# One product per pair of heads and one sum per sequence on VectorE, in a cross-attention kernel

## The reference, cut to what matters

```python
xn = (input - mu) * rsqrt(var + EPS) * gamma + beta        # per sequence
q, kv = Wq @ xn + bq, Wkv @ context + bkv                  # 8 heads
att = softmax(q^T k * c ** -0.5)                           # 256 x 256 per head
y = att @ v
out = input + Wo @ y + bo
```

## Time and profile before

| What | us |
|---|---|
| Three runs: lowest, median, highest | 228.17, 229.04, 229.39 |
| Profiled execution, first to last instruction (span) | 228.2 |
| TensorE busy, in the profiled execution | 208.6 |
| VectorE busy | 199.3 |
| ScalarE busy | 181.1 |
| GpSimd busy | 160.3 |

### The profile page before, as it was taken

How to read it: one execution, slowest core, us unless ns; L and a number is a source line. 1 busy time by engine, 2 the same in 40 slices (tenths; PEclk the granted TensorE clock), 3 DMA queues, 4 the chain that set the end, 5 groups by cost and what they waited for, 6 DMA issues and landing times.

```text
span 228.2 us, 7194 instructions
## 1 busy us (share of the span) xinstructions
PE 208.6 (91%) x2511; PEld 179.9 (79%) x2511; DVE 199.3 (87%) x589; ACT 181.1 (79%) x371; POOL 160.3 (70%) x157
## 2 busy tenths in 40 slices
PE   6968878799999999999999998999999999999872
PEld 6857757588888798889888887888888888887761
DVE  3589987879898999899999999999999998989765
ACT  2374586787889988898889888989897979888880
POOL 5135185777987877789788887789686869776460
PEclk9975897999999999999999999999999999999998
DMA  5964137480767566566665665656657656442000
GB/s 134 261 272 93 27 82 174 107 184 14 164 141 160 131 153 142 132 141 151 140 153 122 160 151 121 151 127 154 142 127 166 149 133 143 93 94 62 13 3 23
DMA packets 31090, 29.04 MB, mean 127 GB/s; under 512 B 4240, under 2 KB 29840, under 8 KB 31056
## 3 DMA queue, kind: packets, MB, share of 16 engines
q1 hardware_dynamic: 30224, 28.07, 52.4%
q10 hardware_dynamic: 832, 0.53, 1.0%
HBM read 3.80 MB, written 1.05 MB: 21 GB/s over the span
## 4 chain that ended last, share of the span: by engine, by line
PE 41%; POOL 20%; issue 13%; ACT 11%; DVE 11%; ACTq 2%; POOLq 0%; DVEq 0%
POOL p_lo L773 19%; PE ps_sc L522 6%; PE ps_max L546 6%; PE ps_sc L523 5%; PE ps_z L479 4%; ACT p_full L678 4%; DVE neg_max L894 4%; ACT p_hi L675 3%; PE ps_z L481 3%; PE ps_z L480 3%; PE ps_z L414 3%; PE ps_m L589 2%; PE ps_t L497 2%; PE ps_m L590 2%; DVE z_sum L910 2%
## 5 line engine op out<-in xcount | busy, mean ns | idle before, releaser
L773 POOL TENSOR_TENSOR p_lo<-p_full,p_hi 128x512 f16<-128x512 f32 x122 | 139.9, 1163 | 42.3 <-ACT p_full L678 41.2
L675 ACT ACTIVATE p_hi<-ps_sc 128x512 f16<-128x512 f32 x128 | 77.9, 608 | 18.3 <-PE ps_sc L523 15.9
L894 DVE TENSOR_REDUCE neg_max<-ps_max 128x2 f32<-128x512 f32 x128 | 85.9, 677 | 6.9 <-PE ps_max L546 6.8
L678 ACT ACTIVATE p_full<-ps_sc 128x512 f32<-128x512 f32 x128 | 78.7, 615 | 0.0
L522 PE MATMUL ps_sc<-t_a,c_seq 128*128 128x256 f32 x256 | 71.2, 300 | 3.5 <-issue 2.6
L523 PE MATMUL ps_sc<-t_b,c_seq 65*128 65x256 f32 x256 | 67.3, 284 | 0.0
L479 PEld LDWEIGHTS ps_z<-u_hi,p_hi 128*128 128x128 f16 x512 | 46.4, 97 | 12.8 <-issue 8.2
L479 PE MATMUL ps_z<-u_hi,p_hi 128*128 128x65 f16 x512 | 53.0, 195 | 2.2 <-DVE p_lo L930 1.9
L522 PEld LDWEIGHTS ps_sc<-t_a,c_seq 128*128 128x128 f32 x256 | 49.2, 192 | 5.9 <-issue 4.6
L480 PE MATMUL ps_z<-u_lo,p_hi 128*128 128x64 f16 x512 | 52.8, 193 | 0.0
L481 PE MATMUL ps_z<-u_hi,p_lo 128*128 128x65 f16 x512 | 52.7, 194 | 0.0
(11 more groups left out here) (108 smaller groups left out, 233.9 us busy)
## 6 DMA issues: line engine op xcount, KB each, us to landing
t_a<-t_a SPq DMA_DIRECT2D x90, 128.0 KB, 2.4
t_b<-t_b SPq DMA_DIRECT2D x30, 128.0 KB, 2.5
x_seq<-x_hi SPq DMA_DIRECT2D x15, 128.0 KB, 2.4
c_pad<-c_hi SPq DMA_DIRECT2D x30, 64.0 KB, 2.1
c_seq<-c_hi SPq DMA_DIRECT2D x15, 128.0 KB, 2.4
x_res<-x_tiles SPq DMA_DIRECT2D x4, 256.0 KB, 6.7
out<-x_res SPq DMA_DIRECT2D x16, 64.0 KB, 2.0
x_seq<-x_lo SPq DMA_DIRECT2D x15, 64.0 KB, 2.1
```

What stands on the lines that cost most here:

```text
L675: nc.scalar.activation(p_hi[:, buf, :, :].rearrange("p t s -> p (t s)"), scores, ACT.Exp).then_inc(act_phi, 1)
L678: nc.scalar.activation(p_full[:, head % 2, :], scores, ACT.Exp).then_inc(act_p, 1)
L773: nc.gpsimd.tensor_tensor(p_lo[:, buf, :, :].rearrange("p t s -> p (t s)"), p_full[:, head % 2, :], p_hi[:, buf, :, :].rearrange("p t s -> ...
L894: nc.vector.tensor_reduce(to, ps_max[:, unit % 2, :].rearrange("p (t s) -> p t s", t=KT), X, ALU.max, negate=True).then_inc(dve_max, 1)
```

## The change

Per pair, VectorE multiplies all four blocks by their reciprocals in one instruction, with each reciprocal broadcast over 64 elements, and writes the results to a new tile `z_heads`, in which the eight heads of one output element lie side by side. Behind the last pair's product, one reduction over these eight gives `z_sum`. A new semaphore, `dve_zpart`, counts the products; `dve_zsum` now counts sequences. TensorE's value products wait for the product of the pair that had their bank, and no longer for its addition. The last pair's reduction waits for the four products and for the transpose of two sequences before.

```diff
+        z_heads = sb("z_heads", [P, 2, KT * C, H], fp32)
...
-                    need(pe, dve_zsum, (m * PAIRS + first // 2 - 1) * 2 * KT)
+                need(pe, dve_zpart, m * PAIRS + first // 2 - 1)
...
-                    for k in range(2):
-                        head = first + k
-                        for qt in range(KT):
-                            total, part, scale = z_sum[:, m % 2, qt, :], sums[:, qt, k, 0:C], inv_sum[:, pair % 2, qt * 2 + k:qt * 2 + k + 1]
-                            if head == 0:
-                                nc.vector.tensor_scalar(total, part, scale, 0.0, ALU.mult, ALU.add).then_inc(dve_zsum, 1)
-                            else:
-                                dve.wait_ge(dve_zsum, (m * H + head - 1) * KT + qt + 1)
-                                nc.vector.scalar_tensor_tensor(out=total, in0=part, scalar=scale, in1=total, op0=ALU.mult,
-                                                               op1=ALU.add).then_inc(dve_zsum, 1)
...
+            def add_values(m, first):
...
+                dve.wait_ge(dve_inv, m * PAIRS + pair + 1)
+                need(dve, dve_zsum, m - 1)
+                to = z_heads[:, m % 2, :, first:first + 2].rearrange("p (t c) k -> p t k c", t=KT)
+                nc.vector.tensor_tensor(to, sums[:, :, :, 0:C], inv.broadcast_to([P, KT, 2, C]), ALU.mult).then_inc(dve_zpart, 1)
+                if first == H - 2:
+                    need(dve, pe_y, m - 1)
+                    dve.wait_ge(dve_zpart, (m + 1) * PAIRS)
+                    nc.vector.tensor_reduce(z_sum[:, m % 2, :, :].rearrange("p t c -> p (t c)"), z_heads[:, m % 2, :, :], X,
+                                            ALU.add).then_inc(dve_zsum, 1)
```

```diff
+                reduce_max(n + 2, 2)
+                p_low(n, 7)
+                u_low(n + 1, 1)
```

More of the change, by code:

```diff
@@ L317, in run, with run_cycles, turn_of, fresh @@
                     step(n, h)
+        def run_cycles(step, cycle):
+            for n in range(-1, FIRST_CYCLE):
+                for h in range(H):
+                    step(n, h)
+            for n in range(FIRST_CYCLE - 1, N + 2):
+                cycle(n)
+        def turn_of(m, k):
+            return k if m == 0 else PAIRS + 2 * (m - 1) + k
+        def fresh(done, kind, index, within=True):
+            if not within or index < done.get(kind, 0) or kind == 't' and index >= PAIRS + 2 * (N - 1):
+                return False
+            done[kind] = index + 1
+            return True
         def chunk(c):
@@ L446, in transpose_max @@
             def transpose_max(m, part):
+                if not fresh(done, 'mt', m + 1 if m else part, m < N):
+                    return
                 rows = H * KT
@@ new lines, in values @@
+            def values(m, first):
+                if not fresh(done, 'values', m * PAIRS + first // 2, 0 <= m < N):
+                    return
+                bank = first // 2 % 2
+                if first == 0:
+                    pe.wait_ge(dve_ulo, 2 * (m + 1))
+                if m == 0 and first < 4:
+                    pe.wait_ge(dve_tlo, T_EARLY)
+                need(pe, dve_zpart, m * PAIRS + first // 2 - 1)
+                lo_done(pe, m, first)
+                lo_done(pe, m, first + 1)
+                for head in (first, first + 1):
+                    buf = head % P_BUFS
+                    for qt in range(KT):
+                        qs = slice(qt * P, (qt + 1) * P)
+                        z0 = (qt * 2 + head % 2) * Z_W
+                        for kt in range(KT):
+                            u_h, u_l = u_hi[:, m % 2, kt, head, 0:Z_W], u_lo[:, m % 2, kt, head, :]
+                            mm(ps_z[:, bank, z0:z0 + Z_W], p_hi[:, buf, kt, qs], u_h, start=(kt == 0), stop=False)
+                            mm(ps_z[:, bank, z0:z0 + C], p_hi[:, buf, kt, qs], u_l, start=False, stop=False)
+                            last = mm(ps_z[:, bank, z0:z0 + Z_W], p_lo[:, buf, kt, qs], u_h, start=False, stop=(kt == KT - 1))
+                    last.then_inc(pe_av, 1)
@@ new lines, in turn_of_t @@
+            def turn_of_t(m, k):
+                turn = turn_of(m, k)
+                if not fresh(done, 't', turn):
+                    return
+                q = m % 2
+                if m == 0 or k == 0:
+                    x_ready(pe, m)
+                if m == 0 and k % 2 == 0:
+                    pe.wait_ge(pool_ahi, 2 * (k // 2 + 1))
+                    pe.wait_ge(dve_alo, k // 2 + 1)
+                if turn == 3:
+                    pe.wait_ge(dve_bo, 2)
+                need(pe, dve_tlo, t_bank_free(turn))
+                bank = t_bank(turn)
+                for j in range(2):
+                    first = (2 * k + j) * 2 * C if m == 0 else (4 * (2 * k + j) + 1) * C
+                    mm(bank[:, j * S:(j + 1) * S], a_hi_cols[:, first:first + 2 * C], x_seq[:, q, 0, :], start=True, stop=False)
+                    last = mm(bank[:, j * S:(j + 1) * S], a_lo_cols[:, first:first + 2 * C], x_seq[:, q, 1, :], start=False, stop=True)
+                last.then_inc(pe_t, 1)
@@ new lines, in maxima @@
+            def maxima(m, unit):
+                if not fresh(done, 'max', m * H + unit, 0 <= m < N):
+                    return
+                q, bank = m % 2, unit % 2
+                need(pe, dve_max, m * H + unit - 1)
+                if m == 0:
+                    if unit == 0:
+                        c_ready(pe, m)
+                    if unit < 2:
+                        pe.wait_ge(dve_alo, unit + 1)
+                    if unit % 2 == 0:
+                        pe.wait_ge(act_thi, unit // 2 + 1)
+                    for qt in range(KT):
+                        last = mm(ps_max[:, bank, qt * S:(qt + 1) * S], t_a[:, q, unit, qt * P:(qt + 1) * P], c_seq[:, m % C_BUFS, 0, :],
+                                  start=True, stop=True)
+                else:
+                    if unit == 0:
+                        pe.wait_ge(dma_cpad[q], 32 * fills(m))
+                    if unit % 4 == 0:
+                        pe.wait_ge(act_thi, PAIRS + 2 * (m - 1) + unit // 4 + 1)
+                    head, qt = unit // 2 * 2, unit % 2
+                    last = mm(ps_max[:, bank, :], t_a[:, q, head, qt * P:(qt + 1) * P], c_pad[:, q, :, :].rearrange("p k s -> p (k s)"),
+                              start=True, stop=True)
+                last.then_inc(pe_s1, 1)
@@ L472, in step @@
-                    for head in (first, first + 1):
-                        buf = head % P_BUFS
-                        for qt in range(KT):
[L475 to L482, removed]
@@ L484, in step @@
-                for turn, m, k in t_at(n, h):
[L485 to L499, removed]
@@ L550, in step @@
[L550 to L557, removed]
+                    values(*e)
+                for turn, m, k in t_at(n, h):
+                    turn_of_t(m, k)
```

385 lines of the change are left out of this document (243 added, 142 removed).

## The result

The changed kernel takes **233.69 us** (median of four runs, 232.81 to 234.73); the kernel before, with a fourth run added, 229.21 (228.17 to 232.14). The ratio is **1.022 [1.017, 1.027]**. The forecast was 230.6, within 228.0 to 236.5: right in sign and inside its range, but 3.1 us short. The profiled execution of the changed kernel took 233.2, with a span of 231.4 against 228.2; the mean granted clock of TensorE is 0.966 against 0.965, so the clock explains nothing.

A forecast was written before the change was run, and what follows sets the result against it. Bound: the loop transpose, ScalarE, u_lo, VectorE's maximum, TensorE, eighth maximum, transpose. Loop 1.0 - 0.3, start +0.5, end +0.4 give +1.6 us: span 228.2 to 229.8, plus 0.84 makes 230.6 us, range 228.0 to 236.5.

The forecast's parts named there:

- The 0.84 of the prediction: Whole run: median of the runs before, 229.04 us, lies 0.84 above the profiled span of 228.2; added to the forecast span.
- The product, 0.42 us: VectorE's new 256-element product per pair: priced at 0.42 us from u_lo's row and the reductions' slope, bounds 0.28 to 0.69.
- a rival with a chance of 0.17: Scattered writes: product writes eight elements apart take a second cycle, 0.27 us more each, some 238 us; chance 0.17.
- VectorE's way, +0.39 against 0.26 of slack: VectorE from u_lo to the eighth maximum: grows 0.39 us against 0.26 slack, so the transpose comes 0.13 later per sequence.
- the 4.42 us from the transpose to `u_lo`: First half of a sequence, through scores and ScalarE's exponentials: 4.42 us that VectorE could not shorten.
- The sign, slower with a chance of 0.56: Whole kernel against the kernel before: slower 0.56, same within 0.5% 0.32, faster 0.12.
- The wait before the transpose, "longer by some 0.3": TensorE's wait before L458, transpose of the eight maxima, 0.40 us on average: longer by some 0.3 per sequence.
- the 0.19 won at `ps_max`: TensorE's wait for VectorE's maximum before a ps_max product: 0.19 us won, then waited again at the transpose.
- Eight intervals at +0.13, five others at -0.3 together: Thirteen intervals between transposes: eight lose 0.13 us each, +1.0; five paced by waits such as DMA loads gain 0.3 together.
- The start, +0.5: First sum over heads, before the transpose at 54.16: chain grows 0.82 us but starts 0.3 earlier, +0.5.
- The end, +0.4: End of run: p_lo before u_lo wins 0.4 us, last pair with its sum loses 0.8, together +0.4.
- VectorE's time, "down by some 7 us": VectorE's work over the run: 0.47 us less per sequence, sixteen times, so down by some 7 us.

The follow-up runs named there:

- pairs together: Changed kernel with z_heads holding a pair's two heads side by side, pairs in blocks (writes step 8 bytes): 228.39 us, 1.000 to the kernel before.
- Heads outermost: Changed kernel with z_heads laid out heads outermost, so the product writes contiguously and the sum reads at 512 bytes: 240.48 us, 1.054 to the kernel before.
- dense operand: Changed kernel with a dense tile of ones replacing the product's broadcast reciprocals, scaling by row sums left out: 234.82 us, one run.
- order alone: Changed kernel's order of work, with the four 64-element instructions per pair of the kernel before: 229.19 us, 1.003 to the kernel before.
- where the sum comes later: Changed kernel with the sum over heads moved ahead of u_lo of the second half: 228.70 us, 0.995 to before; with pairs together also, 225.21 us, 0.986.
- the last one: Changed kernel with both the layout of pairs together and the sum over heads moved ahead of u_lo of the second half: 225.21 us, 0.986 to before.

## Why the prediction was right in sign and short in size

**The 3.1 us that are missing.** The terms of the sum account for 1.6 of them. Between the two profiled executions the span grew by 3.2 us, not by 1.6: the eight intervals by 2.96 for the 1.0 forecast, the five in which the scores waited before by -0.05 for -0.3, the start by -0.54 for +0.5, the end by 0.83 for +0.4. The other 1.5 us are no term of the sum. A time on record is about 1.8 us longer than its span (233.2 against 231.4), so the execution that was profiled before, with a span of 228.2, took about 230.0, some 1.0 above the median of 229.04; the one profiled of the changed kernel lies 0.5 below its median. The 0.84 of the prediction compares a span with times and hides this.

**The product, 0.42 us: the term that failed.** The prediction took the slope of the reductions and noted a dearer product "if the scattered writes need a second cycle each", as its upper bound of 0.69 and as a rival with a chance of 0.17. The runs put the price at 0.628, 0.83 ns per element above the packed product, and show that the step of the writes is the cause: 0.415 where the writes are contiguous, 0.416 at a step of 8 bytes, 0.632 with the step kept and the broadcast gone. The Trainium skill, Advanced Engine Details and Errata, section SBUF Cachelines, asks for "at least two hits on a cacheline" of 16 bytes; the runs agree at three steps (8 bytes free, 32 and 512 dear), and a step of 16 bytes was not tried. The prediction quoted it as evidence that no row showed, and chose the reading side's row: what the new instruction has in common with a known row was priced, and what it does not was left to a rival. The forecast should have leaned towards that rival, whose time of 238 was too long in its turn: 0.21 came of its 0.27, and the five intervals to which it gave 1.8 us lost nothing.

**VectorE's way, +0.39 against 0.26 of slack.** The mechanism holds, with three sizes to correct. Divide the interval at the maximum that follows `u_lo` and a reciprocal (154.98 before, 155.46 in the changed kernel). Before, it starts 5.12 after the transpose, then 5.77 pass to the eighth maximum, then 0.75 to the next transpose. The timelines of ScalarE, TensorE and VectorE of the kernel before show where the first part comes from (ACTq is ScalarE issuing a DMA):

```profile
150.80 0.25 ACT L648 ACTIVATE neg_max_rows<-ps_m 16x128 fp32r<-16x128 f32 x1
151.08 0.51 ACTq L658 DMA_DIRECT2D t_b<-neg_max_rows  x1
151.13 0.28 PE L523 MATMUL ps_sc<-t_b,c_seq 65*128 65x256 f32 x1
...
151.69 0.60 ACT L675 ACTIVATE p_hi<-ps_sc 128x512 f16<-128x512 f32 x1 [0.64 <-PE ps_sc L523]
...
154.98 0.66 DVE L894 TENSOR_REDUCE neg_max<-ps_max 128x2 f32<-128x512 f32 x1
```

In the changed kernel the three parts are 5.01, 6.34 and 0.72, with pairs together 5.00, 6.00 and 0.72.

- The middle part grows by 0.57. The first product takes 0.46 for 0.77, the second with its sum 1.88 for 0.77: +0.80, less the slack of 0.26, is 0.54, and 0.03 lies in the instructions between. The forecast had 0.13. Of the difference, 0.12 is the first product; 0.29 is the second, 0.21 for the product itself, 0.07 because the sum starts 0.11 and not 0.04 behind its end, and 0.01 for the sum; the 0.03 is the rest.
- With the packed product the middle part grows by 0.23: 0.33 and 1.66 for 0.77 each. The step of the writes is thus 0.34 of the 0.57, and with 0.35 the whole distance between the intervals of the two kernels (12.07 and 11.72).
- The prediction said that the 4.42 us from the transpose to `u_lo` "holds nothing that VectorE could shorten". It fell to 4.18. Before, ScalarE issues its DMA until 151.59 and takes the next exponential 1.83 after the transpose; in the changed kernel, as its timeline shows, that comes 1.59 after it:

```profile
151.12 0.53 ACTq L742 DMA_DIRECT2D t_b<-neg_max_rows  x1
...
151.72 0.28 PE L559 MATMUL ps_sc<-t_b,c_seq 65*128 65x256 f32 x1
...
152.04 0.60 ACT L765 ACTIVATE p_hi<-ps_sc 128x512 f16<-128x512 f32 x1 [0.95 <-PE ps_sc L559]
```

  The score product that this exponential needs ends 1.55 after the transpose in both (151.41 and 152.00). The issue ends 1.73 after its transpose before, and 1.20 after it in the changed kernel (151.65). So the profile's label (PE) names the releaser of the second line and not of the first: before, ScalarE's own issue held the exponential up. A later transpose waits less for ScalarE, and gives some of its lateness back. In the intervals that only the loop sets, this fits all eight traces: the exponential starts 0.04 behind the score product or some 0.10 behind the issue, whichever is later. Heads outermost and dense operand have 4.18 to `u_lo` too, pairs together 4.17 to 4.26, order alone 4.42 to 4.46 as before; where the sum comes later, the transpose is early again and the exponential back at 1.84, 0.10 behind the issue. That ScalarE's issue is the cause is read from the timelines, not tried by itself. Of the 0.24, 0.13 goes at the maximum that divides the interval, which now waits for TensorE's product (155.24 plus 0.09 would have been possible, it starts at 155.46); 0.11 stays.

So the interval grows by 0.57 - 0.11 - 0.03 = 0.43, not by 0.13. That the kernel with pairs together lands at 11.72, beside 11.77, owes something to two small errors of opposite sign (+0.10 in the middle part, -0.15 around it).

**The sign, slower with a chance of 0.56.** Part of it is luck. The kernel with the prices that the prediction took is pairs together, and it is not slower: 1.000 [0.996, 1.005], where the forecast's +1.6 us would have been 1.007. VectorE's way overruns its slack there as forecast (11.72 against 11.64), but the thirteen intervals come to the sum of before (154.33 and 154.38). That the changed kernel is clearly slower comes from the product's price, which the prediction had left to the rival.

**The wait before the transpose, "longer by some 0.3".** It is 0.63 longer, and by the prediction's own sum: the 0.19 won at `ps_max`, plus the growth of the interval, with 0.43 in the place of 0.13. That the wait at `ps_max` would go held for the most part (2.8 to 1.0).

**Eight intervals at +0.13, five others at -0.3 together.** Eleven of the thirteen are now at 12.04 to 12.10 and the other two at 12.21 and 12.39, where they ran from 11.64 to 12.34. The five in which the scores waited before changed by -0.05 together, the other eight grew by 2.96. The changed interval runs over the load waits, so those sequences lose nothing, and the loss is 2.91 instead of 13 x 0.43 = 5.6. That the five would differ, and by little, was right; the growth of the eight was not.

**The start, +0.5.** It came out at -0.54, but that interval, the one with the first sum over heads, runs from 12.4 to 15.9 us over the kernels of this study (13.80 before, 13.24 in the changed kernel), and no single profile can give its sign. **The end, +0.4,** was +0.83: the last pair, from product to the sum's end, takes 1.95 (226.52 to 228.47) for the 0.86 of before, +1.09 and not +0.8. Of the 0.4 to be won ahead of it, 0.29 shows: its product starts 15.61 after the last transpose, where the first addition started 15.90 after it. With the dense operand, the same instructions have 15.96, so one profile does not show this gain for sure.

**VectorE's time, "down by some 7 us".** It rose by 2.7. The product took 0.21 more 64 times, 13 us; as the next instruction starts up to 0.17 before the product's end (156.52 against 156.06 + 0.63), 9.0 of this shows in the busy time. With pairs together VectorE is busy 193.0, 6.3 less than before, so the prediction's count was sound and the product's price alone was wrong. That this relief is worth nothing where it lies held: with pairs together the kernel has 6.3 us less VectorE work and the time of before. The rule that fewer chained VectorE operations are better (the Trainium skill, VectorE: DVE Perf Modes, section Rules for kernel authors) is not borne out by the changed kernel, which has 413 for 589 and is 2.2% slower, and is borne out by the last one, which has 413 too and is 1.4% faster; what lies between is the step and the place.

## What to carry to other kernels

Price a new instruction by its writing side as much as by its reading side: a row with the same inputs says nothing of an output that steps over memory, and when a layout makes one side contiguous by scattering the other, look for one that gives both sides two neighbours at a time. When work is collected into one longer instruction, place it where its engine idles each time round, not where its last input happens to come; here the same 1.2 us cost 0.40 to 0.56 us less per sequence in the second place than in the first, in the intervals that only the loop sets. And test a loop's "fixed" part by asking which engine paced it, since a part that another engine paces moves when the loop does.

## What the runs showed of the hardware

- A VectorE instruction with 256 results written at a step of 32 bytes takes 0.628 us, at 8 bytes 0.416, contiguous 0.415. A sum that reads 1024 elements at a step of 512 bytes takes 2.00 us, at a step of 4 bytes 1.220, and in neighbouring pairs 1.220. The surcharge, 0.83 ns per element written at 32 bytes and 0.76 per element read at 512, is about the same; side and step were not varied apart.
- Broadcasting the second operand of this product costs nothing against a dense one (0.628 and 0.632).
- On ScalarE, an exponential behind a DMA issue of 0.51 us starts 0.10 behind the end of that issue (151.59, then 151.69), though the score product that it reads had ended 0.28 before its start (ends of matmuls are modelled).
- A dependent sum starts 0.11 us behind the end of its product (158.64 + 0.63, then 159.38; with packed writes 156.90 + 0.41, then 157.42), while an independent successor starts before the end (156.52, with the product ending at 156.69); the prediction had taken 0.04 from a dependence between two engines.
